# Two attention steps without their DMAs, and mask and score products earlier in TensorE's order, in a macaron block on one core

## The reference, cut to what matters

```python
h = shift_token(x)
q, k, v = jnp.split(h @ wqkv, 3, axis=-1)          # 8 heads of 64
q = l2norm(q) * qs; k = l2norm(k) * ksc
q, k = rotary_xpos(q, k)                           # q*cos*scale + rotate_half(q)*sin*scale
o = local_attention(q, k, v)                       # windows of 64, each sees itself and the one before
x = x + o @ wo
h = layernorm(shift_token(x)) @ w1                 # two halves a, g
x = x + (a * gelu(g)) @ w2 + b2
```

## Time and profile before

| | us |
|---|---|
| median of 3 runs (1102.56 to 1109.77) | 1103.98 |
| the profiled execution | 1103.43 |
| its span, first to last instruction | 1101.60 |

### The profile page before, as it was taken

The page is one execution under the profiler, slowest core; times in us unless marked ns, Lnnn a source line. Parts: engine busy times, 40 slices in busy tenths (PEclk is TensorE's granted clock), DMA queues, the critical chain, the costliest instruction groups (busy, mean ns, idle before and its releaser), DMA issues.

```text
span 1101.6 us, 27125 instructions
## 1 busy us (share of the span) xinstructions
PE 1020.7 (93%) x9596; PEld 673.7 (61%) x9596; DVE 733.4 (67%) x1689; ACT 685.0 (62%) x1329; POOL 527.4 (48%) x392
## 2 busy tenths in 40 slices
PE   4899999999998998899999999998989998889997
PEld 1455555555555366355555555555589995568997
DVE  1788787787876574687787787787674442775442
ACT  3687687686683682677686686684516664825661
POOL 2655665665542543555445445442554550463451
PEclk9999999999998999999999999999989999989999
DMA  5775554444434700554344344343522222012224
GB/s 183 182 180 130 130 150 99 115 117 116 111 92 88 90 2 2 136 128 105 94 102 117 93 102 117 93 102 78 189 69 60 66 69 82 25 58 62 63 68 130
DMA packets 89716, 110.05 MB, mean 100 GB/s; under 512 B 20369, under 2 KB 74385, under 8 KB 88817
## 3 DMA queue, kind: packets, MB, share of 16 engines
q1 hardware_dynamic: 82160, 91.17, 34.6%
q0 software_dynamic: 4544, 9.35, 2.4%
q10 hardware_dynamic: 2880, 7.81, 2.3%
HBM read 62.66 MB, written 12.07 MB: 68 GB/s over the span
## 4 chain that ended last, share of the span: by engine, by line
PE 74%; ACT 8%; DVE 6%; issue 4%; DMA 3%; POOL 3%; SPq 1%; ACTq 0%; DVEq 0%; POOLq 0%
PE banks L648 9%; PE banks L1049 7%; PE banks L1039 6%; PE banks L736 5%; PE banks L697 5%; PE banks L722 5%; PE banks L680 4%; PE banks L729 4%; PE banks L836 4%; PE banks L792 3%; PE banks L781 3%; PE banks L705 3%; PE banks L656 2%; PE banks L615 2%; PE banks L669 2%
## 5 line engine op out<-in xcount | busy, mean ns | idle before, releaser
L2207 POOL TENSOR_TENSOR arena<-arena 128x1024 f32<-128x1024 f32 x64 | 150.9, 2357 | 253.5 <-DVE arena L1798 253.5
L2196 POOL TENSOR_TENSOR arena<-arena 128x1024 f32<-128x1024 f32 x64 | 154.5, 2414 | 70.8 <-ACT arena L1307 66.8
L1297 ACT ACTIVATE arena<-banks,arena 128x512 f32<-128x512 f32 x128 | 80.8, 682 | 103.6 <-PE banks L729 103.0
L648 PE MATMUL banks<-arena 128*128 128x512 f32 x256 | 135.5, 616 | 4.4 <-DVE arena L1689 3.7
L2186 POOL DMA_INDIRECT moe_outs<-arena x78 | 81.4, 1043 | 94.9 <-DVE arena L2052 87.3
L1532 ACT ACTIVATE arena<-banks,arena 128x128 f32<-128x128 f32 x312 | 89.0, 370 | 56.0 <-PE banks L1039 55.9
L1790 DVE TENSOR_REDUCE arena<-banks 128x4 f32<-128x512 f32 x128 | 82.4, 686 | 56.5 <-PE banks L680 56.2
L2179 POOL DMA_INDIRECT moe_rows<-arena x64 | 63.8, 997 | 86.7 <-DVE arena L1770 68.7
L1798 DVE TENSOR_TENSOR arena<-arena 128x1024 f32<-128x1024 f32 x64 | 78.0, 1218 | 22.2 <-DMA arena<-arena 22.2
L1049 PE MATMUL banks<-arena 128*128 x624 | 85.4, 279 | 7.1 <-ACT arena L1532 6.5
L729 PEld LDWEIGHTS banks<-arena 128*128 128x128 f32 x512 | 60.3, 142 | 39.0 <-issue 31.7
(11 more groups left out here) (233 smaller groups left out, 2023.3 us busy)
## 6 DMA issues: line engine op xcount, KB each, us to landing
arena<-arena SPq DMA_DIRECT2D x256, 128.0 KB, 3.3
arena<-rstd SPq DMA_DIRECT2D x128, 256.0 KB, 4.2
arena<-moe_rows SPq DMA_DIRECT2D x78, 64.5 KB
arena<-in_mw SPq DMA_DIRECT2D x2, 2048.0 KB, 11.3
arena<-moe_outs SPq DMA_DIRECT2D x16, 256.0 KB, 4.9
arena<-in_rot ACTq DMA_DIRECT2D x12, 256.0 KB, 3.9
arena<-in_wa ACTq DMA_DIRECT2D x2, 1026.0 KB, 6.2
arena<-ssm_a SPq DMA_DIRECT2D x4, 512.0 KB, 6.5
```

The costliest lines, as they stand in the source:

```text
L648: mm(bank[k], w_qkv[d][:, w0:w0 + P], (YA, YM)[d][:, c * C:(c + 1) * C], start=True, stop=True).then_inc(proj, 1)
L2196: nc.gpsimd.tensor_tensor(TA[:, n % 2], RAW2 if second(s) else RAW, ROTV[:, :, 0, c * C:(c + 1) * C], ALU.mult).then_inc(cos_done, 1)
L2207: nc.gpsimd.tensor_tensor(TA[:, n % 2], TA[:, n % 2], TB, ALU.add).then_inc(rot_sum, 1)
```

## The change

In steps 0 and 1 of each run of F the swap and the spreading of 1/norm are done without DMAs:

- `turn`: two products with a permutation matrix (`turned`, in the place of the unused `flip`) put the swapped q and k into banks 4 and 5; DVE's rotate reads them there. `square_sum_spread`: two full-width products put the sums of squares, already spread over each head's partitions, into banks 2 and 3; ACT's Ln and Exp run over 1024 columns straight into RS or RS2. DVE's normalise waits for that Exp (ss_rstd).
- SP skips steps 0 and 1. DVE instead of POOL adds cosine and sine parts of step 0.
- masks of step 0 wait besides for the rotate and the Ln of step 1 (banks 3 and 4).
- Tile 1's centre moves from step 1 to step 0, its variance (now in bank 7) behind step 0's `turn`, its square and root in ACT to step 0, its `shifted` in DVE to step 2, behind the first normalise.
- Products that nobody reads: 18 on a zeroed tile before the constants land; 4 behind the centre of tile 0 (in run 1 after a wait for the router's copy, wrc), 5 behind its variance, 2 behind the centre of tile 1. The 10 and 8 of run 1 go.

In steps 2 to 7 masks(s-2) and scores(s-2) stand right behind project(s, 1), ahead of transpose_out, values and square_sum. From step 8 on the order is as before. The waits for the two tables of S are merged into one semaphore.

```diff
-        LN_CEN, LN_VAR = (4, 6, 7, 7), (5, 5, 2, 2)
-        LN_STEP = {1: 1, 4: 2, 5: 3}
+        LN_CEN, LN_VAR = (4, 6, 7, 7), (5, 7, 2, 2)
+        LN_STEP = {4: 2, 5: 3}
...
                     for step in range(STEPS):
                         n = STEPS * run + step
+                        if step < 2:
+                            continue
                         sp.wait_ge(copied, 2 * n + 2)
...
+            def warm_zeros(to, n):
+
+                pe.wait_ge(block_done, 1)
+                for _ in range(n):
+                    mm(bank[to][:, 0:P], QF[:, 0:P], QF[:, 0:P], start=True, stop=True)
...
                     after(pe, pt_evac, 2 * n)
+                    if s == 0:
+                        pe.wait_ge(sin_done, n + 2)
+                        pe.wait_ge(ss_log, n + 2)
...
+                def turn(s, n):
+
+                    pe.wait_ge(copied, 2 * n + 2)
+                    if s == 0:
+                        need(pe, ln_log, norm0 + 1)
+                    else:
+                        pe.wait_ge(sin_done, n)
+                    for k in range(2):
+                        last = mm(bank[4 + k], turned, (RAW, RAW2)[s][:, k], start=True, stop=True)
+                    last.then_inc(swap_mm, 1)
+
+                def square_sum_spread(s, n):
+
+                    pe.wait_ge(sq_done, n + 1)
+                    after(pe, ss_log, n)
+                    for k in range(2):
+                        last = mm(bank[2 + k], heads_sum, SQ[:, k * C:(k + 1) * C], start=True, stop=True)
                     last.then_inc(ss_mm, 1)
...
                     project(s, 1)
-                    if s == 0 and run:
-                        warm(6, 8)
+                    if s == 0:
+                        first_centred(norm0, 1, run)
+                        warm(7, 2)
...
-                    if s == 1:
-                        first_centred(norm0, 1, run)
+                    if 2 <= s < 2 * HP:
+                        masks(s - 2, n - 2)
+                        scores(s - 2, n - 2)
                     if s >= 4:
                         transpose_out(s - 4, n - 4, s)
                     if s >= 3:
                         values(s - 3, n - 3, 0)
                         if s < STEPS:
                             values(s - 3, n - 3, 1)
-                    if s < STEPS:
+                    if s < 2:
+                        square_sum_spread(s, n)
+                        turn(s, n)
+                        if s == 0:
+                            first_variance(norm0, 1)
+                    elif s < STEPS:
                         square_sum(s, n)
-                    if s == 1:
-                        first_variance(norm0, 1)
-                    if s >= 2:
+                    if s >= 2 * HP:
                         masks(s - 2, n - 2)
                         scores(s - 2, n - 2)
...
+            warm_zeros(7, 18)
             pe.wait_ge(cst_in, 16)
...
                     first_centred(norm0, 0, run)
+                    if run:
+                        pe.wait_ge(wrc, 18)
+                    warm(7, 4)
                     first_variance(norm0, 0)
-                    if run:
-                        warm(6, 10)
+                    warm(7, 5)
                     ffn(norm0, run)
...
+                def inverse_norm_spread(s, n):
+
+                    act.wait_ge(ss_mm, n + 1)
+                    if s == 0:
+                        need(act, ln_out, norm0 + 1)
+                        after(act, unit_done, n)
+                    to = (RS, RS2)[s]
+                    A(to, two_banks(2), ACT.Ln, scale=2.0 ** SS_SHIFT, bias=tiny_c).then_inc(ss_log, 1)
+                    act.wait_ge(ss_log, n + 1)
+                    A(to, to, ACT.Exp, scale=-0.5, bias=unshift_c).then_inc(ss_rstd, 1)
...
-                    TT(TB, SWAP2 if second(s) else SWAP, ROTV[:, :, 1, c * C:(c + 1) * C], ALU.mult).then_inc(sin_done, 1)
+                    swap = two_banks(4) if s < 2 else SWAP2 if second(s) else SWAP
+                    TT(TB, swap, ROTV[:, :, 1, c * C:(c + 1) * C], ALU.mult).then_inc(sin_done, 1)
+                    if s == 0:
+                        dve.wait_ge(sin_done, n + 1)
+                        dve.wait_ge(cos_done, n + 1)
+                        TT(TA[:, n % 2], TA[:, n % 2], TB, ALU.add).then_inc(rot_sum, 1)
...
                         normalise(s - 2, n - 2)
+                    if s == 2:
+                        norm_chunks(norm0, shifted, [1])
```

More of the change, by code:

```diff
@@ L96, in shape_constants @@
     spare = 2.0 * T + i[:, None]
-    cols = [ident, centre, mean, heads, flip, taps, decays, expert, back,
+    cols = [ident, centre, mean, heads, turned, taps, decays, expert, back,
             np.full((P, 1), LN_EPS), np.full((P, 1), 2.0 ** (SS_SHIFT - 84)),
@@ L147, in macaron_kernel @@
         work = top[0]
-        ident, centre, mean, heads_sum, flip = [CST[:, k * P:(k + 1) * P] for k in range(5)]
+        ident, centre, mean, heads_sum, turned = [CST[:, k * P:(k + 1) * P] for k in range(5)]
         o = 5 * P
@@ L273, in macaron_kernel @@
         outs_dram = nc.dram_tensor("moe_outs", [2 * T + NT * P, DM], F32, kind="Internal")
-        cst_in, mask_in, ssm_in, toeplitz_in, tables_out, wout_in = [sem(n) for n in (
-            "cst_in", "mask_in", "ssm_in", "toeplitz_in", "tables_out", "wout_in")]
+        cst_in, mask_in, ssm_in, ssm_tables_in, tables_out = [sem(n) for n in (
+            "cst_in", "mask_in", "ssm_in", "ssm_tables_in", "tables_out")]
         e_in = [sem(f"e_in_{k}") for k in range(2)]
@@ L286, in macaron_kernel @@
         x_base = sem("x_base")
-        mask_done, pool_init, x_ffn, x_ssm, x_unit = [sem(n) for n in (
-            "mask_done", "pool_init", "x_ffn", "x_ssm", "x_unit")]
+        block_done, pool_init, x_ffn, x_ssm, x_unit = [sem(n) for n in (
+            "block_done", "pool_init", "x_ffn", "x_ssm", "x_unit")]
         e_done, u_mm, u_evac, u_evac_dve, a64_done, state_zero, state_mm, state_scan = [sem(n) for n in (
@@ L482, in _ @@
                         sp.wait_ge(ss_rstd, n + 1)
-                        if n >= 2:
+                        if step >= 4:
                             rs_landed(sp, n - 2)
+                        elif run:
+                            rs_landed(sp, n - 4)
                         sp.dma_start(rstd_dram.ap()[n % 2], SRSTD[0:P:16]).then_inc(rs_out, 16)
-                        sp.wait_ge(rs_out, 16 * (n + 1))
+                        sp.wait_ge(rs_out, 16 * travelled(n + 1))
                         after(sp, unit_done, n + 1 - earlier_use(step))
                         rs_to = RS2 if second(step) else RS
-                        if step == 0:
-                            need(sp, ln_out, norm0 + 1)
                         for e in range(2):
@@ L706, in square_sum @@
                                   start=True, stop=True)
+                    last.then_inc(ss_mm, 1)
+                def turn(s, n):
[12 more added lines that the diff above has]
+                        last = mm(bank[2 + k], heads_sum, SQ[:, k * C:(k + 1) * C], start=True, stop=True)
                     last.then_inc(ss_mm, 1)
@@ L1300, in copy_out @@
                     d = s // (HP * NCH)
-                    if n >= earlier_use(s):
+                    if s in (2, 3):
+                        act.wait_ge(swap_mm, 2 * run + s - 1)
+                    elif n >= STEPS or s >= 4:
                         swap_landed(act, n - earlier_use(s))
@@ L1322, in inverse_norm @@
                     act.wait_ge(ss_log, n + 1)
-                    after(act, rs_out, 16 * n)
+                    after(act, rs_out, 16 * travelled(n))
                     A(SRSTD, SLOG, ACT.Exp, scale=-0.5, bias=unshift_c).then_inc(ss_rstd, 1)
@@ L1777, in normalise @@
                     hp = s % HP
-                    rs_landed(dve, n)
+                    if s < 2:
+                        dve.wait_ge(ss_rstd, n + 1)
+                    else:
+                        rs_landed(dve, n)
                     dve.wait_ge(rot_sum, n + 1)
@@ L1793, in rotate @@
                     c = s // HP % NCH
-                    swap_landed(dve, n)
+                    if s < 2:
+                        dve.wait_ge(swap_mm, 2 * run + s + 1)
+                    else:
+                        swap_landed(dve, n)
                     if run == 0 and s < HP * NCH and s % HP == 0:
@@ L2144, in unit @@
                 rank(1, 3)
+            nc.vector.memset(QF[:, 0:P], 0.0).then_inc(block_done, 1)
             dve.wait_ge(cst_in, 16)
```

38 lines of the change are left out of this document (24 added, 14 removed).

## The result

| | us |
|---|---|
| before, median of 4 runs | 1104.54 |
| after, median of 4 runs (1122.91 to 1124.85) | 1124.43 |
| ratio, 95% interval | 1.0189 (1.0155 to 1.0222) |
| profiled execution of after, its span | 1122.91, 1120.8 |

What follows compares the result with a forecast made beforehand. PE's unbroken chain from step 8 was taken as the bound, so delay reaching it lasts to the end. Terms -3.4 + 2.8 + 9.2 + 9.7 = +18.3 on 1103.43 gave 1121.7 us, range 1110 to 1129.

Steps and rivals of the forecast that it cites:

- The sum: Whole kernel: -3.4 + 2.8 + 9.2 + 9.7 = +18.3 us.
- part 2: Masks and scores moved ahead in steps 2 to 7: a new loop costs +9.2 us in run 0, +9.7 in run 1.
- part 1: Steps 0 and 1 on chip, up to the first scores of both runs: -0.6 us.
- Part 1, run 0: Start of run 0: first scores at 30.7 us against 34.07, -3.4 us.
- Part 1, run 1: Start of run 1: masks before first scores end at 455.2 us against 452.35, +2.8 us.
- Part 2, scores 0 to 2: From scores 0 to scores 2: no change, the same work ends those steps in both orders.
- Part 2, four intervals: Scores 2 to scores 6: loop through PE, ScalarE, VectorE takes 11.8, 11.8, 11.5, 12.3, together 47.4 us, against 38.2 and 37.7.
- Caught up: Rival: behind step 8 PE has room and later steps close the gap, 1103 to 1105 us; chance 6%.
- Early scores hide VectorE's work: Rival, steps 3 to 7: pieces behind the scores fill PE's idle time, up to -4.9 per run, 1093 us; chance 6%.
- Half the loop: Rival: the loop's waits overlap with others counted singly, ScalarE's above all, 1112 us; chance 7%.
- The clock falls as well: Rival: new PE gaps before step 0's projection and in steps 3 to 7 drop the clock, +4, 1126 us; chance 15%.
- The signs named ahead: Intervals 11 to 12.5 us; PE idle before scores and centres; ScalarE idle 2 to 3 us before the sums' Ln.

Runs made afterwards that it cites:

- e1: Changed kernel with masks and scores back behind the sums in steps 2 to 7, steps 0 and 1 still on chip; 1099.52 us, ratio to before 0.9962.
- e2: Kernel before with only the new order of masks and scores in steps 2 to 7; 1133.73 us, ratio 1.023.
- e3: Changed kernel with the sums of squares of steps 2 to 7 ahead of masks and scores, transposes and values still behind; 1109.49 us, ratio 1.0036.
- e5: Changed kernel with transposes and values ahead of masks and scores in steps 2 to 7, only the sums behind; 1108.60 us, ratio 1.0046.
- e7: Changed kernel with masks and scores ahead in steps 2 and 3 only; 1102.66 us, ratio 0.9984.
- e8: e1 without the 18 zero products ahead of the constants; 1101.85 us, ratio 0.9993.
- e4: Changed kernel with ScalarE evacuating the transposed output ahead of Ln and Exp of the sums in steps 4 to 7; 1113.14 us, ratio 1.007.
- e9: Changed kernel with VectorE's shift of tiles 2 and 3 one step later, behind the next normalise; 1119.93 us, ratio 1.014.
- e6: e1 with 13 zero products for 18 and run 1's tile 0 warm-ups not waiting for the router's copy; 1101.22 us, ratio 0.9981.

## Why the prediction was right, point by point

**The sum: +18.3, measured +19.2 by the spans.** The mechanism was right, a ring closed by the new order, and e1 and e2 show that the order alone brings it. That the sum came within 1 us is partly luck: part 2 was 6.3 us too small (18.9 for 25.2), part 1 was 2.2 too high (-0.6 for -2.8), and 3.2 went away in pieces that the sum has at nothing (-0.5 + 0.1 - 2.8).

**Part 1, run 0: -3.4, measured -3.8.** Right by two errors that cancel. The centre behind the zero products was to start at 6.5 and started at 8.20; from the projection to the first scores the sum had 18.1 us and the trace has 16.2, because each pair of products in a dense stream (four passes) took 1.72 to 1.82 us from start to start, not the isolated 1.98. In e3, e5 and e7 the same 18 products ended near 7.2, so this end is no constant. Nor do the zero products give run 0 the 1.5 us of its projection, which the path has in: without them (e8) it took 1.98 too.

**Part 1, run 1: +2.8, measured +1.0.** Mis-sized by the same isolated durations, here with nothing to cancel them: the projection started 4.98 us behind the warm-ups' start (439.16 to 444.14), as predicted (432.06 to 437.1), and the first scores 16.23 behind it where my sum had 18.1. The wait for the router's copy was named rightly and costs 1.2. The true price of the on-chip steps in run 1 is seen only in the old order (e1), 26.00 - 23.21 = 2.8; in the changed kernel the early scores of step 2 hide 1.8 of it (from projection to first scores 16.2 us; 18.0 in e1 and, in run 0, in e3, where the sums stand ahead of masks and scores).

**Part 2, scores 0 to 2: none, measured -0.5 and +0.1.** Right.

**Part 2, four intervals: 47.4, measured 50.5.** The ring was the right one: e5 took exactly its two pieces out, e4 took out ScalarE's three but not values and sums as I had written, and e9 cut the ring at VectorE, where another closed 1.0 to 1.4 us shorter. Sizes in steps 4 and 5: predicted 3.0 + 1.57 + 5.90 + 1.33 = 11.8; the chain has 3.39 + 1.58 + 5.90 + 1.38 = 12.25. So the term that was too small is the 3.0 behind the normalise, above all scores at 0.89 and transposes at 0.44. I misread those rows. A piece of the chain leaves out what overlaps the piece before it, and the row of 0.89 counts 21 of the 32 score products; whole, the same groups take 1.05 (98.34) and 0.60 us (95.92) in PE's timeline. In the ring the scores start only behind a wait, when the masks are done, and the chain has 1.11 for them and 0.59 for the transposes. Step 6 was to take 11.5 and took 13.3, of which some 1.5 are the clock (granted 0.61 from 72.3 to 76.5 us; scores 1.98 for 1.11, transposes 1.05 for 0.59), as e4 and e9 show with 11.71 and 11.82; step 7 12.3 and 12.7.

**The rivals.** *Caught up* is refuted: the 8.07 us of step 8 are 8.12 at 340 us. The Trainium skill (Trainium Kernel Development and Optimization, Performance Expectations) calls weight-load busy time a good measure of how near the limit a kernel is; weight loads are busy 21.49 of 40 us there, and a delay of 8 us was not made up all the same, so here that measure did not show whether PE had room. *Early scores hide VectorE's work* is refuted by PE's idle 0.7 to 1.3 us ahead of the scores, released by the normalise. *Half the loop*: no, the pieces do hang end to end. *The clock falls as well* came in part: one fall in each run at step 6 (granted clock 0.61 from 72.3 and 0.55 from 502.4 us), some 3 us together.

**The signs named ahead** were there: the scores' wait on the normalise, the centre's on the evacuation, and ScalarE idle 2.1 to 2.6 us (4.4 at step 6) before the Ln of the sums. Of the intervals, 11 to 12.5 by forecast, those of steps 4 and 5 lie inside (12.25 and 12.26) and those of steps 6 and 7 above (13.31 and 12.71). The first scores of run 1 came 21.3 us after the router's copy ended, not 23.

## What to carry to other kernels

In an order written by hand, what is put ahead of its neighbours on an in-order engine hands its own wait to all of them: before moving an instruction forward, find what it waits for and what of the pieces behind it feeds that wait a step later. If that closes a ring, each piece costs its full length per turn, however empty the engines are, and the ring can be added up from the rows. A piece taken out gives back its length only until another path is the longest, as e3, e4 and e9 show. Take the durations of a ring from rows behind a wait and those of a full stream from start to start, and see that a row counts the whole group.

## What was not expected of the hardware

- The zero products. The same 36 passes took 5.92 to 7.20 us in the nine kernels that start with them, one execution each. Up to 5.00 us some 18 of them take 3.84 us, 0.21 each; the passes of later warm-ups took 0.13. The Trainium skill (TensorE: Matmul & The Clock Gate, Part 1) says that the number of slow products at a start changes from run to run; these rows agree.
- The granted clock stands at 1.00 in the first 10 us of all these kernels, over the slow passes too. In the kernel before it also reads 1.00 from 14.00 to 17.60, over the projection of 3.48 us, where e6 has 0.58 over one of 3.32. So at the start of an execution these rows don't tell the level; the durations do.
- The projection of step 0 starts after 1.84 to 1.85 us of idle PE in run 0 of every kernel with the on-chip steps, and ran at either level (1.98 us, 3.32 in e6). So did that of run 1, whose start is the same code in e1 and e7: its four passes took 1.99 us after 1.84 us of idle in e1 and 3.45 after 1.85 in e7, at a granted clock of 0.56 (431.1 to 434.6).
